# A Winograd FFN with dynamic mixing: the bias is put into PSUM by ScalarE, experts and mixing one product later

## The chip, the cores and the metric

One core of one Trainium2 chip runs the whole kernel. The metric is the device time of one launch in microseconds. The same program was run three times before the change: 948.63 us median, 948.12 to 948.87.

## The reference, cut to what matters

```python
# conditional mixing: x is (128, 64, 1024); att is (128, 8), from a small MLP on cond_128
agg_w = einsum('bk,koi->boi', att, weight)         # one 64x64 mixing matrix for each of 128 batch rows
agg_b = att @ bias_k                               # one bias for each batch row and channel
c     = einsum('boi,bih->boh', agg_w, x) + agg_b[:, :, None]
# FFN on the 8192 rows of c, 1024 columns each
logits = c @ W_router.T                            # 8 experts, top 2
h      = einsum('nd,erd->ner', c, A)               # LoRA, 8 experts of rank 16
out    = c @ W_base.T + b_base + 2 * einsum('ner,eor->no', h * combine, B)
result = x + out
```

The kernel multiplies first and mixes afterwards: `z = x @ [A | W_router | W_base].T` is 1160 columns wide, and the mixing matrix is applied to z. The bias then enters as `agg_b * col_sum`, where `col_sum` holds the sum of each of the 1160 weight columns. That product, of one value for each row and one for each column, has to be added to every mixed tile.

## The kernel before, in words

All matmuls work on fp32 split in two parts (`_hi` and `_lo`), three matmuls for one product. x is held as 64 tiles of 128 rows (two batch rows each), and two tiles make a unit: 32 units, 0 to 31. For a unit the two tiles and the two halves of the contraction make a 2x2 block matrix, and so do the weights: seven block products by Winograd's scheme (`A11`, `A12`, `S2`, `S1`, `S3`, `S4`, `A22`), each of 24 matmuls of 290 columns, in two parts. `S1` to `S4` are sums of blocks of x that VectorE makes.

The work of one unit is spread over two turns of the loop. `mix_upper(u)` at the end of turn u mixes the upper tile (side 0) of unit u into PSUM banks 4 to 6 (`O_BANK`), nine matmuls. Turn u+1 then routes it (`route`, top 2 of 8, `gate` on ScalarE for the exponential), transposes the weighted LoRA vector `hw` (`transpose_hw` on TensorE for side 0; for side 1 on TensorE in turns 1 to 4 and 31, called early, otherwise 16 block transposes on VectorE, `transpose_lower`), splits it (`hwT_high` on ScalarE, `hwT_low` on VectorE), and adds the experts (`experts`, nine matmuls into the same banks). VectorE then adds the banks to the tile's rows of `x_sb` (`result`), which frees the banks for the lower tile (`mix_lower`, side 1), and SP stores the tile.

The order on each engine is written out by hand: TensorE, ScalarE (act), VectorE (dve), GpSimd (pool) and SP each have a function `unit(u)` that lists the steps of a turn, with semaphores between the engines. Each engine takes its instructions in that order. Turn 1 is a case of its own (`first`, and `unit_1` on VectorE): there the last weight blocks `T3` and `T4` are still split, ScalarE and VectorE each with one long instruction (`split_weight`), beside the unit's other work.

The steps that the change and the prediction touch:

- `mixed` (L462 to L469) starts each bank with `start=True`; `mix_upper` and `mix_lower` (L472 to L486) wait for `out_done`, the end of `result`.
- `put_biases` (L1047 to L1051) on VectorE fills a tile's rows of `x_sb` with `col_sum * agg_b + bias_out`, when the store of the tile before has landed (`stored`); GpSimd then starts a DMA that adds x to it (`add_x`, L924 to L928).
- `route` (L992 to L1020) adds the bias to the 136 columns of logits and LoRA itself, with two `scalar_tensor_tensor`.
- The sums of products: `save` (ScalarE, PSUM to SBUF) and `add_acc` (VectorE) make `sum1`, `sum2`, `sum3`; they are split into `z_hi` (ScalarE) and `z_lo` (VectorE) by `z11_*`, `z12_*`, `z22_*`, `z21_*`. `mixed(0, 1)` in `mix_upper` needs `z12_low`.

Of the kernel before, what the change touches and what calls it, by code (L numbers as in the profile page):

```python
# [14 lines left out]
P = 128  # L15
# [87 lines left out]
def build(nc, x, xT, small, keep, mix_w, wide, b_base, bT, out):  # L103
# [8 lines left out]
    with ExitStack() as ctx:  # L112
# [10 lines left out]
        agg_b = sb("agg_b", [P, TILES])  # L123
        ones_r = sb("ones_r", [P, P], F32R)
# [54 lines left out]
        lower_hwT = sb("lower_hwT", [P, P])  # L179
# [47 lines left out]
        biased = sem("biased")  # L227
        mix_hi_done = sem("mix_hi_done")
# [22 lines left out]
        lower_hwT_made = sem("lower_hwT_made")  # L251
# [171 lines left out]
        def _(pe):  # L423
# [48 lines left out]
            def mix_upper(u):  # L472
                pe.wait_ge(mix_lo_done, tile_no(u, 0) + 1)
                pe.wait_ge(z11_lo_done, u + 1)
                mixed(0, 0).then_inc(ar_mm, 1)
                pe.wait_ge(z12_lo_done, u + 1)
                mixed(0, 1)
                mixed(0, 2).then_inc(mixed_mm, 1)

            def mix_lower(u):  # L480
                pe.wait_ge(mix_lo_done, tile_no(u, 1) + 1)
                pe.wait_ge(z22_lo_done, u + 1)
                pe.wait_ge(out_done, tile_no(u, 0) + 1)
                mixed(1, 0).then_inc(ar_mm, 1)
                mixed(1, 1)
                mixed(1, 2).then_inc(mixed_mm, 1)  # L486
# [114 lines left out]
            def unit(u, par, first=False, early=False):  # L601
# [9 lines left out]
                if first:  # L611
                    pe.wait_ge(b_lo_done, 1)
                experts(u - 1, 0)
# [5 lines left out]
                mix_lower(u - 1)  # L619
                pe.wait_ge(z11_summed, u + 1)  # L620
                pe.wait_ge(x_lo_done, splits(u, "S1"))
                product(b, "S1", True)
                pe.wait_ge(u2_saved, u)
# [7 lines left out]
                experts(u - 1, 1)  # L631
                pe.wait_ge(p5_saved, u)
                pe.wait_ge(x_lo_done, splits(u, "S4"))
                product(b, "S4", False)
                pe.wait_ge(z22_summed, u + 1)
# [4 lines left out]
                pe.wait_ge(out_done, tile_no(u - 1, 1) + 1)  # L640
# [57 lines left out]
        def _(act):  # L698
# [16 lines left out]
            def lower_hwT_high(u):  # L715

                act.wait_ge(lower_hwT_made, u * (BLOCKS * BLOCKS) - (BLOCKS_FROM - 2) * (BLOCKS * BLOCKS))
                act.wait_ge(out_mm, tile_no(u, 1))
                nc.scalar.copy(hwT_hi[:], lower_hwT[:]).then_inc(hwT_hi_done, 1)
# [107 lines left out]
            def unit(u, par, first=False, early=False):  # L827
# [8 lines left out]
                mix_high(u, 0)  # L836
                act.wait_ge(product_mm, products(u, "A11"))
                save(sum1, a, p1_saved)
                x_high("S3")
                hwT_high(2 * u - 1 if early else u + (BLOCKS_FROM - 1))  # L840
# [3 lines left out]
                act.wait_ge(s_made, sums(u, "S4"))  # L844
                act.wait_ge(product_mm, products(u, "A12"))
                x_high("S4")
                act.wait_ge(product_mm, products(u, "S2"))
                save(sum2, a, u2_saved)
                x_high("A22")
                act.wait_ge(mixed_mm, tile_no(u - 1, 1) + 1)  # L850
                mix_high(u, 1)
                if first:
                    split_weight(T4, t4_stage)
                gate(u - 1, 1)
                act.wait_ge(product_mm, products(u, "S1"))
                save(sum3, b, p5_saved)
                if early:
                    hwT_high(2 * u)
                else:
                    lower_hwT_high(u - 1)  # L860
                z11_high(u)
# [5 lines left out]
                x_high("A12")  # L867

# [12 lines left out]
            x_high("S3")  # L881
            hwT_high(LAST + (BLOCKS_FROM - 1))
            act.wait_ge(s_made, sums(u, "S4"))
# [25 lines left out]
        def _(pool):  # L909
# [34 lines left out]
            for side in range(2):  # L944
                add_x(LAST, side)

        @block.vector
        def _(dve):
# [43 lines left out]
            def route(u, side, bank=O_BANK):  # L992
# [44 lines left out]
            def result(u, side):  # L1037
# [4 lines left out]
                nc.vector.tensor_tensor(x_sb[:, side, res], ps[:, O_BANK, at], x_sb[:, side, res], ALU.add)  # L1042
# [77 lines left out]
            def unit_1():  # L1120
# [3 lines left out]
                route(0, 0)  # L1124
# [23 lines left out]
                result(0, 1)  # L1148
# [176 lines left out]
```

## Time and profile before

| what | value |
|---|---|
| median of 3 runs | 948.63 us |
| profiled execution | 948.32 us, its span 946.6 us |
| TensorE matmul busy | 939.5 us, 99% |
| VectorE busy | 777.5 us, 82% |
| ScalarE busy | 331.5 us, 35% |
| GpSimd busy | 92.8 us, 10% |
| granted TensorE clock, mean | 0.998 |

The span runs from the first to the last instruction of the profiled execution; the 1.7 us between it and the execution's time lie around it. Matmul busy times overlap (a matmul starts while the one before still drains), so the distance from one start to the next is what a matmul costs. A busy share near 100% means that there are no gaps to close.

### The profile page before, as it was taken

What the parts mean: (1) busy time and instruction counts of PE and PEld (TensorE: products, weight loads), DVE (VectorE), ACT (ScalarE), POOL (GpSimd) and SP (SyncE); (2) the same over time, 40 slices, a digit from 0 to 9 for tenths busy, and PEclk for the clock granted to TensorE, in tenths of its full rate; (3) what the DMA queues carried; (4) which work ended last, traced back from release to release, by engine and by line L of the source; (5) the groups of instructions that cost most, each with busy time, mean ns of one, the idle gap of its engine ahead of it and who ended that gap; (6) DMA issues with size and microseconds to landing.
All of it is one profiled execution on the core that took longest, in us unless ns stands there. A gap on an engine that the chain in (4) does not pass through costs nothing.

```text
span 946.6 us, 19080 instructions
## 1 busy us (share of the span) xinstructions
PE 939.5 (99%) x6713; PEld 935.7 (99%) x6713; DVE 777.5 (82%) x1970; ACT 331.5 (35%) x675; POOL 92.8 (10%) x139
## 2 busy tenths in 40 slices
PE   9999999999999999999999999999999999999997
PEld 8999999999999999999999999999999999999997
DVE  5987876888888888888888888888888888888885
ACT  6653333233332233342333332333332333332331
POOL 1111001101001101001101001100011010011010
PEclk9999999999999999999999999999999999999999
DMA  8444335444345343345344354343344343454434
GB/s 306 141 114 115 94 111 136 111 118 97 97 123 136 100 126 91 92 134 136 92 134 91 90 136 135 91 119 92 106 136 117 109 98 99 120 136 105 121 91 111
DMA packets 36053, 111.39 MB, mean 118 GB/s; under 512 B 13200, under 2 KB 13456, under 8 KB 31936
## 3 DMA queue, kind: packets, MB, share of 16 engines
q1 hardware_dynamic: 26656, 77.32, 22.3%
q0 software_dynamic: 9376, 33.78, 21.5%
q8 instruction: 14, 0.23, 0.1%
q14 instruction: 7, 0.06, 0.0%
HBM read 75.37 MB, written 35.65 MB: 117 GB/s over the span
## 4 chain that ended last, share of the span: by engine, by line
PE 98%; DMA 1%; SPq 0%; DVE 0%; ACT 0%; issue 0%; DVEq 0%
PE ps L431 25%; PE ps L435 25%; PE ps L433 25%; PE ps L491 9%; PE ps L467 4%; PE ps L465 4%; PE ps L469 4%; DMA w_stage<-in_wide 1%; PE ps L458 0%; PE ps L457 0%; PE ps L514 0%; PE ps L517 0%; SPq L371 0%; SPq L365 0%; DVE w_lo L1056 0%; DVE x_sb L1268 0%
## 5 line engine op out<-in xcount | busy, mean ns | idle before, releaser
L431 PE MATMUL ps<-w_hi,x_hi 128*128 128x290 f32 x1544 | 460.2, 298 | 0.7 <-DVE w_lo L1056 0.3
L433 PE MATMUL ps<-w_lo,x_hi 128*128 128x290 f32 x1544 | 457.8, 297 | 0.0
L435 PE MATMUL ps<-w_hi,x_lo 128*128 128x290 f32 x1544 | 456.9, 296 | 0.0
L431 PEld LDWEIGHTS ps<-w_hi,x_hi 128*128 128x128 f32 x1544 | 291.4, 189 | 2.9 <-DVE w_lo L1056 1.9
L435 PEld LDWEIGHTS ps<-w_hi,x_lo 128*128 128x128 f32 x1544 | 291.3, 189 | 0.0
L433 PEld LDWEIGHTS ps<-w_lo,x_hi 128*128 128x128 f32 x1544 | 291.2, 189 | 0.0
L700 ACT CAST x_hi<-xT_sb 128x512 fp32r<-128x512 f32 x186 | 115.5, 621 | 187.8 <-DVE xT_sb L967 167.3
L951 DVE TENSOR_TENSOR x_lo<-xT_sb,x_hi 128x512 fp32r<-128x512 f32 x186 | 129.0, 694 | 22.5 <-ACT x_hi L700 22.5
L928 POOL DMA_DIRECT2D x_sb<-in_x x64 | 55.5, 867 | 691.9 <-DVE x_sb L1049 691.9
L722 ACT COPY sum<-ps 128x580 f32<-128x580 f32 x96 | 61.6, 642 | 100.2 <-PE ps L435 100.2
L1031 DVE STREAM_TRANSPOSE lower_hwT<-hw 32x32 f32<-32x32 f32 x416 | 84.2, 202 | 12.2
L1049 DVE SCALAR_TENSOR_TENSOR x_sb<-col_sum,agg_b,bias_out 128x1024 f32<-128x1024 f32 x64 | 81.8, 1279 | 1.3 <-ACT col_sum L757 1.3
L431 PE MATMUL ps<-t_hi,x_hi 128*128 128x290 f32 x248 | 74.2, 299 | 0.0
L435 PE MATMUL ps<-t_hi,x_lo 128*128 128x290 f32 x248 | 73.9, 298 | 0.0
L433 PE MATMUL ps<-t_lo,x_hi 128*128 128x290 f32 x248 | 73.3, 296 | 0.0
L970 DVE TENSOR_TENSOR sum<-ps,sum 128x580 f32<-128x580 f32 x92 | 69.5, 755 | 1.4 <-PE ps L435 1.3
L730 ACT CAST z_hi<-sum 128x580 fp32r<-128x580 f32 x31 | 21.0, 678 | 139.0 <-DVE sum L970 139.0
L467 PE MATMUL ps<-z_hi,mix_lo 128*128 128x384 f32 x189 | 64.2, 340 | 0.0
L465 PE MATMUL ps<-z_hi,mix_hi 128*128 128x384 f32 x189 | 64.1, 339 | 0.0
L984 DVE TENSOR_TENSOR z_lo<-ps,z_hi 128x580 fp32r<-128x580 f32 x31 | 23.6, 761 | 48.8 <-ACT z_hi L735 48.8
L469 PE MATMUL ps<-z_lo,mix_hi 128*128 128x384 f32 x189 | 63.5, 336 | 0.0
L1044 DVE TENSOR_TENSOR x_sb<-ps,x_sb 128x776 f32<-128x776 f32 x62 | 59.2, 955 | 0.0
(128 smaller groups left out, 1156.4 us busy)
## 6 DMA issues: line engine op xcount, KB each, us to landing
x_sb<-in_x POOLq DMA_DIRECT2D x64, 512.0 KB, 5.4
result<-x_sb SPq DMA_DIRECT2D x63, 512.0 KB, 5.2
xT_sb<-in_xT SPq DMA_DIRECT2D x31, 1024.0 KB, 4.8
b_sb<-in_wide SPq DMA_DIRECT2D x4, 580.0 KB, 13.0
agg_w_rows<-agg_w SPq DMA_DIRECT2D x1, 2048.0 KB, 7.5
mix<-agg_w_rows SPq DMA_DIRECT2D x124, 16.0 KB, 4.4
w_stage<-in_wide SPq DMA_DIRECT2D x4, 290.0 KB, 5.4
w_stage<-in_wide SPq DMA_DIRECT2D x2, 580.0 KB, 8.0
```

Of the source, the lines that this page charges most:

```text
L431: nc.tensor.matmul(dst, x_hi[:, s, rows], high[:, c, cols], start=first, stop=False, skip_group_check=True)
L433: nc.tensor.matmul(dst, x_hi[:, s, rows], low[:, c, cols], start=False, stop=False, skip_group_check=True)
L435: mm = nc.tensor.matmul(dst, x_lo[:, s, rows], high[:, c, cols], start=False, stop=last, skip_group_check=True)
L465: nc.tensor.matmul(dst, mix_hi[:, side, :], high[:, columns(k)], start=start, stop=False, skip_group_check=True)
L467: nc.tensor.matmul(dst, mix_lo[:, side, :], high[:, columns(k)], start=False, stop=False, skip_group_check=True)
L469: return nc.tensor.matmul(dst, mix_hi[:, side, :], low[:, columns(k)], start=False, stop=True, skip_group_check=True)
L491: mm = nc.tensor.matmul(ps[:, banks[k], at], stat[:], mov[:, res], start=False, stop=True, skip_group_check=True)
L700: nc.scalar.copy(x_hi[:, SLOT[name], :], raw(name)).then_inc(x_hi_done, 1)
L951: nc.vector.tensor_tensor(x_lo[:, SLOT[name], :], raw(name), x_hi[:, SLOT[name], :].bitcast(F32), ALU.subtract).then_inc(x_lo_done, 1)
L970: nc.vector.tensor_tensor(dst[:], acc(first), dst[:], ALU.add).then_inc(done, 1)
L1031: nc.vector.transpose(lower_hwT[there, here], hw[here, there]).then_inc(lower_hwT_made, 1)
L1049: nc.vector.scalar_tensor_tensor(x_sb[:, side, :], col_sum[:, AR:WIDE], agg_b[:, bass.ds(tile_no(u, side), 1)], bias_out[:], ALU.mult, ALU.add
```

## The change

ScalarE takes over what `put_biases` did in turns 1 to 30, and in two places. It fills a tile's rows of `x_sb` with a plain copy of the output bias (`put_out_bias`), and it writes `col_sum * tile bias` into PSUM banks 4 to 6 ahead of the mixing (`seed`, in two instructions, 384 and 776 columns), so that the mixing's matmuls start with `start=False` and add to it. `take_bias` copies the tile's column of `agg_b` for it. `route` then reads logits and LoRA with plain copies. VectorE's first half of `result` signals `head_out`, so that the seed of bank 4 can go ahead of the second half. TensorE's turn has `experts(u - 1, 0)` behind `S2` instead of ahead of it, `mix_lower` behind `S1`, and `experts(u - 1, 1)` behind `S4`. The steps of ScalarE, VectorE and GpSimd are moved to fit. The unit that the prologue mixes (unit 0) and the last one keep the old way of adding the bias (`route(..., False)`, `put_biases`). The diff, without declarations and renames:

```diff
@@ -472,18 +478,25 @@
         pe.wait_ge(z11_lo_done, u + 1)
-        mixed(0, 0).then_inc(ar_mm, 1)
+        pe.wait_ge(head_put, tile_no(u, 0) - 1)
+        mixed(0, 0, start=False).then_inc(ar_mm, 1)
         pe.wait_ge(z12_lo_done, u + 1)
-        mixed(0, 1)
-        mixed(0, 2).then_inc(mixed_mm, 1)
...
-    def mix_lower(u):
+        pe.wait_ge(rest_put, tile_no(u, 0) - 1)
+        mixed(0, 1, start=False)
+        mixed(0, 2, start=False).then_inc(mixed_mm, 1)
...
+    def mix_lower(u, seeded=True):
         pe.wait_ge(mix_lo_done, tile_no(u, 1) + 1)
         pe.wait_ge(z22_lo_done, u + 1)
-        pe.wait_ge(out_done, tile_no(u, 0) + 1)
-        mixed(1, 0).then_inc(ar_mm, 1)
-        mixed(1, 1)
-        mixed(1, 2).then_inc(mixed_mm, 1)
+        if seeded:
+            pe.wait_ge(head_put, tile_no(u, 1) - 1)
+        else:
+            pe.wait_ge(out_done, tile_no(u, 0) + 1)
+        mixed(1, 0, start=not seeded).then_inc(ar_mm, 1)
+        if seeded:
+            pe.wait_ge(rest_put, tile_no(u, 1) - 1)
+        mixed(1, 1, start=not seeded)
+        mixed(1, 2, start=not seeded).then_inc(mixed_mm, 1)
@@ -608,18 +621,18 @@
         product_part(b, "A12", 1, True).then_inc(product_mm, 1)
-        if first:
-            pe.wait_ge(b_lo_done, 1)
-        experts(u - 1, 0)
         pe.wait_ge(p1_saved, u)
...
         product(a, "S2", False)
-        mix_lower(u - 1)
+        if first:
+            pe.wait_ge(b_lo_done, 1)
+        experts(u - 1, 0)
         pe.wait_ge(z11_summed, u + 1)
...
         product(b, "S1", True)
+        mix_lower(u - 1, not first)
         pe.wait_ge(u2_saved, u)
@@ -628,16 +641,15 @@
         product_part(a, "S3", 1, False).then_inc(product_mm, 1)
-        experts(u - 1, 1)
         pe.wait_ge(p5_saved, u)
...
         product(b, "S4", False)
+        experts(u - 1, 1)
         pe.wait_ge(z22_summed, u + 1)
...
         product(a, "A22", False)
-        pe.wait_ge(out_done, tile_no(u - 1, 1) + 1)
         mix_upper(u)
@@ -712,11 +724,32 @@
-    def lower_hwT_high(u):
...
-        act.wait_ge(lower_hwT_made, u * (BLOCKS * BLOCKS) - (BLOCKS_FROM - 2) * (BLOCKS * BLOCKS))
-        act.wait_ge(out_mm, tile_no(u, 1))
-        nc.scalar.copy(hwT_hi[:], lower_hwT[:]).then_inc(hwT_hi_done, 1)
+    def blocks_hwT_high(u, side, blocks):
...
+        act.wait_ge(blocks_made, blocks)
+        act.wait_ge(out_mm, tile_no(u, side))
+        nc.scalar.copy(hwT_hi[:], blocks_hwT[:]).then_inc(hwT_hi_done, 1)
...
+    def put_out_bias(u, side):
...
+        act.wait_ge(stored[side], u * 16)
+        nc.scalar.copy(x_sb[:, side, :], bias_out[:]).then_inc(out_bias_put, 1)
...
+    def take_bias(u, side):
+        nc.scalar.copy(tile_bias[:, side:side + 1], agg_b[:, bass.ds(tile_no(u, side), 1)]
+                       ).then_inc(tile_bias_done, 1)
...
+    def seed(u, side):
...
+        t = tile_no(u, side)
+        act.wait_ge(tile_bias_done, t - 1)
+        act.wait_ge(head_out, t)
+        nc.scalar.activation(ps[:, O_BANK, 0:width(0)], col_sum[:, columns(0)], ACT.Copy,
+                             scale=tile_bias[:, side:side + 1]).then_inc(head_put, 1)
+        act.wait_ge(out_done, t)
+        nc.scalar.activation(ps[:, O_BANK + 1:O_BANK + 3, 0:width(1)],
+                             col_sum[:, CUTS[1]:WIDE].rearrange("p (k n) -> p k n", k=2), ACT.Copy,
+                             scale=tile_bias[:, side:side + 1]).then_inc(rest_put, 1)
@@ -833,38 +866,49 @@
             x_high("S1")
         z22_high(u - 1)
         gate(u - 1, 0)
-        mix_high(u, 0)
         act.wait_ge(product_mm, products(u, "A11"))
         save(sum1, a, p1_saved)
+        if not first:
+            take_bias(u - 1, 1)
+        mix_high(u, 0)
         x_high("S3")
-        hwT_high(2 * u - 1 if early else u + (BLOCKS_FROM - 1))
         if first:
             act.wait_ge(t_made, T_AT["T3"])
             split_weight(T3, t_stage)
-        act.wait_ge(s_made, sums(u, "S4"))
-        act.wait_ge(product_mm, products(u, "A12"))
-        x_high("S4")
+            act.wait_ge(bias_out_in, 16)
+            act.wait_ge(agg_b_done, 2)
+            act.wait_ge(col_sum_done, 2)
+        else:
+            put_out_bias(u - 1, 1)
+        hwT_high(2 * u - 1 if early else u + (BLOCKS_FROM - 1))
         act.wait_ge(product_mm, products(u, "S2"))
         save(sum2, a, u2_saved)
+        act.wait_ge(s_made, sums(u, "S4"))
+        x_high("S4")
         x_high("A22")
-        act.wait_ge(mixed_mm, tile_no(u - 1, 1) + 1)
-        mix_high(u, 1)
         if first:
             split_weight(T4, t4_stage)
-        gate(u - 1, 1)
+        else:
+            seed(u - 1, 1)
         act.wait_ge(product_mm, products(u, "S1"))
         save(sum3, b, p5_saved)
+        gate(u - 1, 1)
+        act.wait_ge(mixed_mm, tile_no(u - 1, 1) + 1)
+        z11_high(u)
+        mix_high(u, 1)
         if early:
             hwT_high(2 * u)
         else:
-            lower_hwT_high(u - 1)
-        z11_high(u)
+            blocks_hwT_high(u - 1, 1, u * (BLOCKS * BLOCKS) - (BLOCKS_FROM - 1) * (BLOCKS * BLOCKS))
+        put_out_bias(u, 0)
+        take_bias(u, 0)
         act.wait_ge(xT_in, u * 16 + 16)
         act.wait_ge(product_mm, products(u, "S3"))
         x_high("A11")
         z12_high(u)
         act.wait_ge(product_mm, products(u, "S4"))
         x_high("A12")
+        seed(u, 0)
     units(act, unit)
     u = LAST
@@ -879,7 +923,10 @@
     x_high("S3")
+    put_out_bias(u - 1, 1)
+    take_bias(u - 1, 1)
     hwT_high(LAST + (BLOCKS_FROM - 1))
+    seed(u - 1, 1)
     act.wait_ge(s_made, sums(u, "S4"))
@@ -923,26 +970,30 @@
-        t = tile_no(u, side)
-        pool.wait_ge(biased, t + 1)
-        pool.dma_start(x_sb[:, side, :], x_tiles[t], accum_op=ALU.add).then_inc(x_in[side], 16)
+        pool.dma_start(x_sb[:, side, :], x_tiles[tile_no(u, side)], accum_op=ALU.add).then_inc(x_in[side], 16)
...
         mix_low(0, side)
+    pool.wait_ge(biased, 1)
     add_x(0, 0)
+    pool.wait_ge(biased, 2)
     add_x(0, 1)
...
         mix_low(u, 1)
+        pool.wait_ge(out_bias_put, tile_no(u, 0) - 1)
         add_x(u, 0)
+        pool.wait_ge(out_bias_put, tile_no(u, 1) - 1)
         add_x(u, 1)
...
         mix_low(LAST, side)
-    for side in range(2):
-        add_x(LAST, side)
+    pool.wait_ge(biased, 3)
+    add_x(LAST, 0)
+    pool.wait_ge(biased, 4)
+    add_x(LAST, 1)
@@ -989,16 +1040,21 @@
-    def route(u, side, bank=O_BANK):
+    def route(u, side, seeded=True, bank=O_BANK):
         t = tile_no(u, side)
...
         logits, lora = slice(ER, AR), slice(0, ER)
-        nc.vector.scalar_tensor_tensor(ar[:, logits], col_sum[:, logits], agg_b[:, bass.ds(t, 1)],
-                                       ps[:, bank, logits], ALU.mult, ALU.add).then_inc(routed, 1)
-        dve.wait_ge(routed, step + 1)
-        nc.vector.scalar_tensor_tensor(ar[:, lora], col_sum[:, lora], agg_b[:, bass.ds(t, 1)],
-                                       ps[:, bank, lora], ALU.mult, ALU.add).then_inc(routed, 1)
+        if seeded:
+            nc.vector.tensor_copy(ar[:, logits], ps[:, bank, logits]).then_inc(routed, 1)
+            dve.wait_ge(routed, step + 1)
+            nc.vector.tensor_copy(ar[:, lora], ps[:, bank, lora]).then_inc(routed, 1)
+        else:
+            nc.vector.scalar_tensor_tensor(ar[:, logits], col_sum[:, logits], agg_b[:, bass.ds(t, 1)],
+                                           ps[:, bank, logits], ALU.mult, ALU.add).then_inc(routed, 1)
+            dve.wait_ge(routed, step + 1)
+            nc.vector.scalar_tensor_tensor(ar[:, lora], col_sum[:, lora], agg_b[:, bass.ds(t, 1)],
+                                           ps[:, bank, lora], ALU.mult, ALU.add).then_inc(routed, 1)
         nc.vector.max(top_val[:], ar[:, logits]).then_inc(routed, 1)
@@ -1039,7 +1095,8 @@
         res, at = out_columns(0)
-        nc.vector.tensor_tensor(x_sb[:, side, res], ps[:, O_BANK, at], x_sb[:, side, res], ALU.add)
+        nc.vector.tensor_tensor(x_sb[:, side, res], ps[:, O_BANK, at], x_sb[:, side, res], ALU.add
+                                ).then_inc(head_out, 1)
         rest = x_sb[:, side, res.stop:D].rearrange("p (k n) -> p k n", k=2)
@@ -1131,73 +1188,68 @@
         dve.wait_ge(p1_saved, 1)
         dve.wait_ge(product_mm, products(1, "A12"))
         add_acc(sum1, b, z11_summed)
+        split_weight(T3, SPLIT_AT["T3"], t_stage)
+        x_low(1, "S3")
         result(0, 0)
-        x_low(1, "S3")
         dve.wait_ge(x_lo_done, splits(1, "A12"))
         make_s4(1)
-        split_weight(T3, SPLIT_AT["T3"], t_stage)
-        route(0, 1)
         x_low(1, "S4")
         x_low(1, "A22")
+        route(0, 1, False)
         hwT_low(0, 1)
         z11_low(1)
         dve.wait_ge(p5_saved, 1)
         dve.wait_ge(product_mm, products(1, "S3"))
         add_acc(sum3, a, z22_summed)
         split_weight(T4, SPLIT_AT["T4"], t4_stage)
-        result(0, 1)
+        dve.wait_ge(xT_in, 32)
+        make_s1(2)
         dve.wait_ge(u2_saved, 1)
         dve.wait_ge(product_mm, products(1, "S4"))
         add_acc(sum2, b, z12_summed)
-        dve.wait_ge(xT_in, 32)
-        make_s1(2)
+        result(0, 1)
         make_s3(2)
+        x_low(2, "A11")
         z12_low(1)
-        x_low(2, "A11")
         x_low(2, "A12")
         dve.wait_ge(x_lo_done, splits(2, "A11"))
-        dve.wait_ge(stored[0], 16)
         make_s2(2)
-        put_biases(1, 0)
     def unit(u, par, first=False, early=False):
         a, b = accumulators(par)
         z21_low(u - 1, b)
         route(u - 1, 0)
         x_low(u, "S2")
+        x_low(u, "S1")
+        hwT_low(u - 1, 0)
         z22_low(u - 1)
-        hwT_low(u - 1, 0)
-        x_low(u, "S1")
-        dve.wait_ge(stored[1], u * 16 - 16)
-        put_biases(u - 1, 1)
         dve.wait_ge(p1_saved, u)
         dve.wait_ge(product_mm, products(u, "A12"))
         add_acc(sum1, b, z11_summed)
-        result(u - 1, 0)
         x_low(u, "S3")
         dve.wait_ge(x_lo_done, splits(u, "A12"))
         make_s4(u)
+        result(u - 1, 0)
         x_low(u, "S4")
+        x_low(u, "A22")
         route(u - 1, 1)
-        x_low(u, "A22")
         if early:
+            z11_low(u)
             hwT_low(u - 1, 1)
         else:
-            transpose_lower(u - 1)
-            hwT_low(u - 1, 1, lower_hwT[:])
-        dve.wait_ge(stored[0], u * 16)
-        z11_low(u)
-        put_biases(u, 0)
+            transpose_blocks(u - 1, 1)
+            z11_low(u)
+            hwT_low(u - 1, 1, blocks_hwT[:])
         dve.wait_ge(p5_saved, u)
         dve.wait_ge(product_mm, products(u, "S3"))
         add_acc(sum3, a, z22_summed)
-        result(u - 1, 1)
         dve.wait_ge(xT_in, u * 16 + 16)
         make_s1(u + 1)
-        make_s3(u + 1)
         dve.wait_ge(u2_saved, u)
         dve.wait_ge(product_mm, products(u, "S4"))
         add_acc(sum2, b, z12_summed)
+        result(u - 1, 1)
+        make_s3(u + 1)
         x_low(u + 1, "A11")
         z12_low(u)
         x_low(u + 1, "A12")
@@ -1213,8 +1265,6 @@
     x_low(u, "S1")
-    dve.wait_ge(stored[1], u * 16 - 16)
-    put_biases(u - 1, 1)
     dve.wait_ge(p1_saved, u)
```

## Rows read from the trace of the kernel before

**Rows 1.** The page: busy time of the engines.
```profile
PE 939.5 (99%) x6713; PEld 935.7 (99%) x6713; DVE 777.5 (82%) x1970; ACT 331.5 (35%) x675; POOL 92.8 (10%) x139
```

**Rows 2.** All waits: waiter, whom for, us in total, times, longest.
```profile
PEld ps L514 <- DVE hw L1020: 0.2, 1, 0.2
```

**Rows 3.** Windows: turn 1, and one steady turn; stretch, busy us by engine, clock.
```profile
48.01:76.72 28.71, 28.71 (x207) 28.71 (x207) 25.02 (x50) 12.79 (x21) 2.73 (x4) 1.00 0.43 114
...
504.68:533.29 28.61, 28.61 (x207) 28.61 (x206) 24.03 (x65) 9.51 (x20) 2.69 (x4) 1.00 0.44 113
```

**Rows 4.** Timeline of ScalarE in turn 1: start us, us long, what.
```profile
51.98 0.62 ACT L700 CAST x_hi<-xT_sb 128x512 fp32r<-128x512 f32 x1
53.15 0.27 ACT L713 CAST hwT_hi<-ps 128x128 fp32r<-128x128 f32 x1 [0.55 <-PE ps L514]
53.31 2.14 ACT L746 CAST t_hi<-w_stage 128x2320 fp32r<-128x2320 f32 x1
...
61.17 2.14 ACT L746 CAST w_hi<-w_stage 128x2320 fp32r<-128x2320 f32 x1
63.20 0.20 ACT L708 ACTIVATE ratio<-top_gap 128x1 f32<-128x1 f32 x1
```

**Rows 5.** Timeline of VectorE in turn 1.
```profile
53.45 0.29 DVE L1035 TENSOR_TENSOR hwT_lo<-ps,hwT_hi 128x128 fp32r<-128x128 f32 x1 [0.80 <-ACT hwT_hi L713]
53.66 0.75 DVE L989 TENSOR_TENSOR z_lo<-sum,z_hi 128x580 fp32r<-128x580 f32 x1
54.32 1.28 DVE L1049 SCALAR_TENSOR_TENSOR x_sb<-col_sum,agg_b,bias_out 128x1024 f32<-128x1024 f32 x1
55.52 0.76 DVE L970 TENSOR_TENSOR sum<-ps,sum 128x580 f32<-128x580 f32 x1
56.26 0.42 DVE L1042 TENSOR_TENSOR x_sb<-ps,x_sb 128x248 f32<-128x248 f32 x1
56.59 0.96 DVE L1044 TENSOR_TENSOR x_sb<-ps,x_sb 128x776 f32<-128x776 f32 x1
57.46 0.68 DVE L951 TENSOR_TENSOR x_lo<-xT_sb,x_hi 128x512 fp32r<-128x512 f32 x1
58.06 0.68 DVE L967 TENSOR_TENSOR xT_sb<-xT_sb 128x512 f32<-128x512 f32 x1
58.66 2.57 DVE L1056 TENSOR_TENSOR t_lo<-w_stage,t_hi 128x2320 fp32r<-128x2320 f32 x1
61.15 0.21 DVE L997 SCALAR_TENSOR_TENSOR ar<-col_sum,agg_b,ps 128x8 f32<-128x8 f32 x1
...
63.44 0.15 DVE L1012 TENSOR_SCALAR scaled_sum<-ratio 128x1 f32<-128x1 f32 x1 [1.06 <-ACT ratio L708]
...
63.84 0.35 DVE L1020 SCALAR_TENSOR_TENSOR hw<-ar,first_w,expert_w 128x128 f32<-128x128 f32 x1
```

**Rows 6.** Timeline of TensorE in turn 1: the transposition of side 1.
```profile
65.58 0.28 PE L514 MATMUL ps<-keep_sb,hw 128*128 128x128 f32 x1
```

**Rows 7.** Timeline of ScalarE: a copy of 1024 columns.
```profile
47.16 1.05 ACT L825 CAST b_hi<-x_sb 128x1024 fp32r<-128x1024 f32 x1
```

**Rows 8.** Timelines of TensorE and its weight loads, steady turn: after the experts; `mixed(0, 1)`.
```profile
526.87 0.29 PE L431 MATMUL ps<-w_hi,x_hi 128*128 128x290 f32 x1
...
533.83 0.34 PE L465 MATMUL ps<-z_hi,mix_hi 128*128 128x388 f32 x1
...
533.65 0.19 PEld L465 LDWEIGHTS ps<-z_hi,mix_hi 128*128 128x128 f32 x1
```

**Rows 9.** Timelines of TensorE and VectorE, last turn: the last experts, and the `result` that waits.
```profile
923.92 0.64 PE L491 MATMUL ps<-b_hi,hwT_lo 128*128 128x248 f32 x3
...
924.66 0.42 DVE L1042 TENSOR_TENSOR x_sb<-ps,x_sb 128x248 f32<-128x248 f32 x1 [0.66 <-PE ps L491]
```

**Rows 10.** Timeline of VectorE, steady turn: the 16 block transposes.
```profile
521.06 3.71 DVE L1031 STREAM_TRANSPOSE lower_hwT<-hw 32x32 f32<-32x32 f32 x16
```

**Rows 11.** Groups by line: the second of ScalarE's two table loads, xcount, busy us, ns.
```profile
L780 ACT ACT_TABLE_LOAD x1 | 1.3, 1283 | 0.0
```

More of the change, by code:

```diff
@@ L123, in build @@
         agg_b = sb("agg_b", [P, TILES])
+        tile_bias = sb("tile_bias", [P, 2])
         ones_r = sb("ones_r", [P, P], F32R)
@@ L178, in build @@
         hw = sb("hw", [P, ER])
-        lower_hwT = sb("lower_hwT", [P, P])
+        blocks_hwT = sb("blocks_hwT", [P, P])
         hwT_hi = sb("hwT_hi", [P, P], F32R)
@@ L227, in build @@
         biased = sem("biased")
+        out_bias_put = sem("out_bias_put")
+        tile_bias_done = sem("tile_bias_done")
+        head_put = sem("head_put")
+        rest_put = sem("rest_put")
+        head_out = sem("head_out")
         mix_hi_done = sem("mix_hi_done")
@@ L250, in build @@
         hwT_mm = sem("hwT_mm")
-        lower_hwT_made = sem("lower_hwT_made")
+        blocks_made = sem("blocks_made")
         hwT_hi_done = sem("hwT_hi_done")
@@ L1023, in route, with transpose_blocks @@
                     expert_w[:].unsqueeze(2).to_broadcast([P, EXPERTS, RANK]), ALU.mult, ALU.mult).then_inc(hw_done, 1)
-            def transpose_lower(u):
-                dve.wait_ge(hw_done, tile_no(u, 1) + 1)
+            def transpose_blocks(u, side):
+                dve.wait_ge(hw_done, tile_no(u, side) + 1)
                 for i in range(BLOCKS):
@@ L1030, in transpose_lower @@
                         there, here = slice(j * BLOCK, (j + 1) * BLOCK), slice(i * BLOCK, (i + 1) * BLOCK)
-                        nc.vector.transpose(lower_hwT[there, here], hw[here, there]).then_inc(lower_hwT_made, 1)
+                        nc.vector.transpose(blocks_hwT[there, here], hw[here, there]).then_inc(blocks_made, 1)
             def hwT_low(u, side, whole=hwT):
@@ L1123, in unit_1 @@
                 z21_low(0, b)
-                route(0, 0)
+                route(0, 0, False)
                 dve.wait_ge(b_hi_done, 1)
@@ L1235, in _ @@
                                     ).then_inc(z21_lo_done, 1)
-            route(u, 0)
+            route(u, 0, False)
             dve.wait_ge(p5_saved, u)
@@ L1262, in _ @@
             low_half(1)
-            route(u, 1, LAST_BANKS[0])
+            route(u, 1, False, LAST_BANKS[0])
             def add_piece(side, k, bank):
```

## The prediction

> **What bounds the kernel.** I read the page first: TensorE is busy for 939.5 of 946.6 us [rows 1], VectorE for 82% and ScalarE for 35%. A busy share can hide small gaps, since matmuls overlap, so next came the windows of single turns: turn 1 takes 28.71 us and a steady turn 28.61, TensorE busy in all of it at a granted clock of 1.00 [rows 3]. A turn issues 168 matmuls of 290 columns, 18 of the mixing and 18 of the experts. From the start of S4 to `mixed(0, 1)` there are 48 of the first kind and 3 of the mixing in 6.96 us [rows 8]; 0.134 us for one of 290 columns and 0.178 for one of the mixing fit it (48 x 0.134 + 3 x 0.178 = 6.97). So a product is 3.21 us, a mixing 1.60, and the experts, which take the rest of the turn, 1.41 each. These are starts back to back. What TensorE idles in the whole span, 7.1 us [rows 1], lies in the prologue and the epilogue, which the change leaves alone. TensorE's own stream sets the time, and the change takes not one matmul out of it: the same products, the same mixing (with or without `start`), the same 38 transpositions. The 1.28 us that each `put_biases` costs VectorE [rows 5] lie beside TensorE throughout. So there is nothing to win, and the question is only whether the new order makes TensorE wait. I give places as time after the start of a turn: 48.01 for turn 1, 504.68 + 1.60 for the steady one.
>
> **Parts at nothing: TensorE's order in a steady turn.** New order: A11 0, A12 3.21, S2 6.54, experts(0) 9.75, S1 11.16, `mix_lower` 14.37, S3 15.97, S4 19.19, experts(1) 22.40, A22 23.81, `mix_upper` 27.02. For each wait I followed the other queues with the durations of before [rows 4, 5, 7] (an instruction's successor starts some 0.1 us ahead of its end: 53.66 to 54.32 for one of 0.75 us).
> ScalarE gains per turn two copies of 1024 columns (1.05 us each [rows 7]), two seeds and two `take_bias` (0.2 each, like the one-column exponential [rows 4]). The trace has no ScalarE write to PSUM. The seeds are bounded by 0.27 (128 columns) and 0.62 (512) for the 384 columns and by 0.62 and 1.05 for the 776 [rows 4, 7]; I take 0.5 and 0.85, straight between the rows. With 5.2 us more ScalarE is busy 14.7 of 28.6 us.
> Seed of the lower tile: the experts' end lets `result` start at 11.16 + 0.27 = 11.43 (the last three experts end at 924.56, VectorE starts 0.10 later [rows 9]; the next product has by then been going for 0.17). Its first half is read by 11.88, its second by 12.75 (0.42 and 0.96 long [rows 5]). Seeds end at 12.4 and 13.6; the weight loads that need them are due at 14.2 and 14.7. Margin 1.8 and 1.1 us. With the upper bounds of the seeds it is 1.7 and 0.9.
> Seed of the upper tile: behind `z12_high` and one x split, 25.05 to 26.5, due at 26.9 and 27.4. Margin about 1.
> `hw` of side 1: routing can start at 15.2 and takes 1.98 (from 61.15 to 64.19 without the 1.06 of its wait [rows 5]), so ends at 17.2; 3.7 us of block transposes [rows 10] to 20.9, `hwT_high` 21.2, due at 22.25: margin 1. `hwT_high` of side 0 is now behind `put_out_bias` and ends at 6.2, due at 9.6. In turns 2 to 4 the transposition on TensorE needs `hw` at 17.44 (17.57 less 0.13 for its weight load): margin 0.2.
> SP and GpSimd: store(0) leaves with `result` at 12.9 instead of 9.7, so the two mix loads behind it (2.2 us) push load_xT to 15.8 (before: 15.1); it lands near 21, its first users are at 22.4. The add of x for side 0 leaves at 22.2 and is wanted a turn later at 11.4; that of side 1 at 6 and is wanted at 24. GpSimd's `mix_low` is queued behind it, and is due at 27. All hidden.
> **The tightest place** is new: `result` of side 1 now stands between the last `add_acc` and `z12_low`. From A22's start: 0.27 to `result`, 0.33 + 0.87 for its halves, 0.60 `make_s3`, 0.60 `x_low`, 0.75 `z12_low` (all from starts [rows 5]), 0.04 to the next engine: 3.46. The weight load of `mixed(0, 1)` is due 3.57 after it (3.21 + 0.54 - 0.18 [rows 8]). Margin 0.1 us. I take no wait. If the chain is 0.1 longer than I think there is none yet; each 0.1 beyond costs 30 x 0.1 = 3 us. A wait that is just missed is paid at its length and no more: in the last turn the weight load of the transposition stood 0.2 us for `hw` [rows 2], and the products behind it kept their pace.
> Last turn: TensorE's order is unchanged. The lower seed ends at 10.4, due at 11.5. Nothing.
>
> **The part that costs: turn 1.** There the moves meet the two weight splits. I follow the chain from 51.98, where ScalarE's queue changes.
> ScalarE: `mix_high` (0.2), x split (0.52), then T3's split from 52.70, now ahead of `hwT_high`. A split holds the queue 2.03 us (61.17 to 63.20 [rows 4]). `hwT_high` starts at 54.73, before 53.15, and ends at 55.00.
> VectorE: `hwT_low` at 55.03 (before 53.45 [rows 5]), then by the starts of before: + 0.21 = 55.24 `z22_low`, + 0.66 = 55.90 `put_biases`, + 1.20 = 57.10 `add_acc`, + 0.68 = 57.78 T3's low half, now ahead of everything, + 2.49 = 60.27 x_low S3, + 0.60 = 60.87 `result`, + 1.20 = 62.07 `make_s4`, ready at 62.75. (The experts of side 0, done at 59.4, and `mix_lower`, which needs `result` done by 62.2, just pass.)
> ScalarE: x split S4 at 62.79 (before 58.78), x split A22 63.31, T4's split 63.83 to 65.86, the save of `sum3` 0.54, and only then `gate` of side 1: 66.40 to 66.60. Before, the gate ran at 63.20 [rows 4].
> VectorE: has routed up to the gate by 65.9, takes `scaled_sum` at 66.64, `hw` 0.40 later, done at 67.39 (0.40 and 0.35 [rows 5]).
> TensorE: the transposition of side 1 stands at the same place as before, since the steps in front are the same: 65.58 [rows 6]. It can start at 67.39 + 0.13 = 67.52 at the latest, about 1.9 us late. Behind it everything has room again (`experts(1)` needs `hwT` 5 us later, and `p5` is saved at 66.5, before S4). Next late is T4's low half, done at 72.8, wanted at 73.8. The 1.9 us stay.
>
> **Sum.** 948.32 (own time of the profiled execution: span 946.6 and 1.7 around it) + 1.9 + 0 = 950.2. The median of the runs lies 0.3 above the profiled execution, so 950.6 in the measure of the runs.
>
> **Rivals.**
> A, turn 1 absorbs the wait: if `gate` or `make_s4` comes 1.9 us earlier than my chain (it has twelve links and two are waits I inferred), the transposition is on time, and the time is 948.6, unchanged: TensorE's stream is the same. For it: margins in all other places. Against it: no link in the chain is short of its wait [rows 4, 5].
> B, `z12_low` misses in every turn: the margin is 0.1 us out of 3.57. From 0.1 us more on it decides. Port or memory contention of `put_out_bias`, the seeds and GpSimd's DMA issue beside VectorE would do it: 0.2 us more is 0.1 of wait in 30 turns, 3 us, beside turn 1: 953.6. Against it: VectorE's durations are steady (0.75 to 0.76 [rows 5] whatever runs beside).
> C, the seeds' function makes ScalarE reload its table between the exponential and the copy. One load is 1.28 us [rows 11], four a turn. The upper seed's second half would then end at 27.8 for 27.4, the routing of side 1 comes later by a load: about 0.35 us a turn, 30 turns: 950.6 + 10.5 = 961. Only two loads stand in the trace, with copies and exponentials mixed throughout; but the copies there are not activations with a scale.
> The Trainium skill (ScalarE: Activation LUTs, "Table sets: the hidden batching unit") says that cheap functions, copy among them, are in every set. By that rule there is no reload, and the trace agrees as far as it goes.
> D, faster: matmuls that run denser beside less VectorE traffic. For it: 0.134 us for 290 columns leaves room in principle. One ns on each of 6400 would give 948.6 + 1.9 - 6.4 = 944. Against it: turns with 25.0 and 24.0 us of VectorE work differ by no more than the 0.1 us of one transposition [rows 3].
>
> **Numbers.** Forecast (turn 1 alone pays) 0.60, A 0.18, B 0.15, C 0.03, D 0.04. 0.2% (1.9 us) is about what a measurement of this kernel can tell from no change, and the forecast of + 1.9 stands on that line: of its 0.60 I give 0.34 to slower, for a longer chain, and 0.26 to within. Slower 0.34 + 0.15 + 0.03 = 0.52, within 0.26 + 0.18 = 0.44, faster 0.04. The range leaves out D and C and takes in A and most of B: 948.2 to 953.8.
>
> **What would show it.** In turn 1 one wait of TensorE of 1.9 us at the transposition of side 1, released by VectorE's `hw`, the gate on ScalarE near 66.4, the turn at 30.6 us. Steady turns at 28.61 with no wait. VectorE's busy time some 60 x 1.28 = 77 us less, ScalarE's up by 150. Wrong would be: waits at `mixed(0, 1)` on `z12_low` (B), table loads in the turns (C), a wait on a seed at the mixing, or turns shorter than 28.6.

## The result

The changed kernel takes 950.77 us (median of 12 runs, 950.27 to 951.27), the kernel before, run beside it, 948.72 (948.12 to 949.42): 2.05 us more, a ratio of 1.002 with an interval of 1.0012 to 1.0028. Forecast were 950.6 us. The kernel is slower, by 0.1 to 0.3%.

The page of the changed kernel: span, and busy time of the engines.

```profile
span 949.3 us, 19345 instructions
...
PE 940.7 (99%) x6713; PEld 936.5 (99%) x6713; DVE 696.2 (73%) x1910; ACT 474.4 (50%) x915; POOL 100.1 (11%) x139
```

Against [rows 1] VectorE has 81 us less work and ScalarE 143 us more, and TensorE has as many instructions as before and waits longer. The page can't say where, the waits can. All waits of TensorE's matmuls and the first of its weight loads, columns as in [rows 2]:

```profile
PE ps L527 <- DVE hw L1076: 1.7, 1, 1.7
PE ps L549 <- POOL ones L957: 1.1, 1, 1.1
PE ps L520 <- ACT hwT_hi L725: 0.4, 1, 0.4
PE ps L437 <- DVE x_lo L1118: 0.3, 1, 0.3
PE ps L437 <- DVE sum L1021: 0.3, 1, 0.3
...
PEld ps L527 <- DVE hw L1076: 2.1, 2, 1.9
```

Behind the prologue one wait is new, the 1.7 us on `hw` (1.9 in the weight loads, whose second wait on `hw`, 0.2 us near the end, stood in the kernel before too [rows 2]). The wait on `x_lo` stands in the prologue, at 11.8 us. The windows of turn 1 and of a steady turn, which answer to [rows 3]:

```profile
48.70:79.67 30.97, 29.13 (x207) 28.69 (x207) 25.32 (x49) 14.83 (x25) 5.57 (x5) 1.00 0.51 122
507.76:536.38 28.62, 28.62 (x207) 28.62 (x206) 21.29 (x63) 14.29 (x28) 2.67 (x4) 1.00 0.43 113
```

Turn 1 takes 31.03 us from start to start of TensorE's first matmuls (48.72 to 79.75), before 28.74 (48.01 to 76.75): 2.29 us more. The steady turn is as long as before, 28.62 to 28.61, with 2.7 us less of VectorE and 4.8 us more of ScalarE in it. The two places in turn 1, from the timeline of the weight loads (the bracket is the idle time before):

```profile
63.34 0.19 PEld L471 LDWEIGHTS ps<-z_hi,mix_hi 128*128 128x128 f32 x1 [0.34 <-issue]
68.50 0.14 PEld L527 LDWEIGHTS ps<-keep_sb,hw 128*128 128x128 f32 x1 [1.94 <-DVE hw L1076]
```

The first is `mix_lower` (the profile names no releaser; VectorE's second half of `result`, which it needs, ends at 63.22), the second the transposition of side 1. ScalarE's timeline of turn 1, for [rows 4]:

```profile
52.86 0.62 ACT L712 CAST x_hi<-xT_sb 128x512 fp32r<-128x512 f32 x1
53.38 2.13 ACT L779 CAST t_hi<-w_stage 128x2320 fp32r<-128x2320 f32 x1
55.41 0.26 ACT L725 CAST hwT_hi<-ps 128x128 fp32r<-128x128 f32 x1
...
64.90 2.13 ACT L779 CAST w_hi<-w_stage 128x2320 fp32r<-128x2320 f32 x1
66.94 0.63 ACT L755 COPY sum<-ps 128x580 f32<-128x580 f32 x1
67.46 0.20 ACT L720 ACTIVATE ratio<-top_gap 128x1 f32<-128x1 f32 x1
```

And VectorE's, for [rows 5]:

```profile
55.70 0.29 DVE L1091 TENSOR_TENSOR hwT_lo<-ps,hwT_hi 128x128 fp32r<-128x128 f32 x1 [2.35 <-ACT hwT_hi L725]
...
58.45 2.70 DVE L1113 TENSOR_TENSOR t_lo<-w_stage,t_hi 128x2320 fp32r<-128x2320 f32 x1
61.08 0.94 DVE L1002 TENSOR_TENSOR x_lo<-xT_sb,x_hi 128x512 fp32r<-128x512 f32 x1
61.95 0.40 DVE L1098 TENSOR_TENSOR x_sb<-ps,x_sb 128x248 f32<-128x248 f32 x1
62.27 0.95 DVE L1101 TENSOR_TENSOR x_sb<-ps,x_sb 128x776 f32<-128x776 f32 x1
...
67.70 0.15 DVE L1068 TENSOR_SCALAR scaled_sum<-ratio 128x1 f32<-128x1 f32 x1 [0.75 <-ACT ratio L720]
...
68.10 0.35 DVE L1076 SCALAR_TENSOR_TENSOR hw<-ar,first_w,expert_w 128x128 f32<-128x128 f32 x1
```

Read from the end: `hw` waits for the gate (67.46), which stands behind T4's split and a save; the split stands behind the split of S4, which waits for `make_s4`; that stands behind T3's low half and `result` on VectorE; and these were held for 2.35 us by `hwT_low`, because `hwT_hi` stands behind T3's split on ScalarE. The spans of the two profiles differ by 2.7 us, the medians by 2.05. The 2.7 us are 0.7 in the prologue (turn 1 starts at 48.72 and not at 48.01; in all eleven profiles it starts between 48.0 and 48.9), 2.3 in turn 1, 0.2 in turns 2 to 30 together, and 0.5 less from the start of turn 31 to the end (39.27 to 39.74). Whether the last one belongs to the change is not shown: the nine profiles in the new order have 39.15 to 39.48 there, the two in the old order 39.62 and 39.74.

### The profile page after: what moved, and what is told of

Read it like the earlier page. It is cut to its first block, busy times and chain, and to the rows that moved or that the text cites. A ratio compares the mean times of both kernels' runs of the same rounds, so it can differ in the third digit from the quotient of the medians.

```text
span 949.3 us, 19345 instructions
## 1 busy us (share of the span) xinstructions
PE 940.7 (99%) x6713; PEld 936.5 (99%) x6713; DVE 696.2 (73%) x1910; ACT 474.4 (50%) x915; POOL 100.1 (11%) x139
## 4 chain that ended last, share of the span: by engine, by line
PE 96%; DVE 1%; DMA 1%; ACT 1%; issue 0%; SPq 0%; DVEq 0%
PE ps L441 25%; PE ps L437 25%; PE ps L439 25%; PE ps L504 9%; PE ps L473 3%; PE ps L475 3%; PE ps L471 3%; DMA w_stage<-in_wide 1%; PE ps L464 0%; PE ps L463 0%; PE ps L527 0%; ACT w_hi L779 0%; PE ps L530 0%; SPq L377 0%; ACT x_hi L712 0%
## 5 line engine op out<-in xcount | busy, mean ns | idle before, releaser
L712 ACT CAST x_hi<-xT_sb 128x512 fp32r<-128x512 f32 x186 | 112.4, 621 | 6.6 <-DVE xT_sb L1018 4.8
L1087 DVE STREAM_TRANSPOSE blocks_hwT<-hw 32x32 f32<-32x32 f32 x416 | 84.4, 203 | 13.1
L1098 DVE TENSOR_TENSOR x_sb<-ps,x_sb 128x248 f32<-128x248 f32 x62 | 25.8, 416 | 85.4 <-PE ps L504 85.2
L968 POOL TENSOR_TENSOR mix_lo<-mix,mix_hi 128x128 fp32r<-128x128 f32 x64 | 50.3, 787 | 302.0 <-ACT mix_hi L716 302.0
L736 ACT COPY x_sb<-bias_out 128x1024 f32<-128x1024 f32 x60 | 62.8, 1047 | 0.0
L750 ACT ACTIVATE ps<-col_sum,tile_bias 128x776 f32<-128x776 f32 x60 | 54.8, 913 | 9.3 <-DVE x_sb L1101 7.5
```

The source lines that it names most:

```text
L712: nc.scalar.copy(x_hi[:, SLOT[name], :], raw(name)).then_inc(x_hi_done, 1)
L736: nc.scalar.copy(x_sb[:, side, :], bias_out[:]).then_inc(out_bias_put, 1)
L1087: nc.vector.transpose(blocks_hwT[there, here], hw[here, there]).then_inc(blocks_made, 1)
```

## The experiments

Unless told otherwise an experiment starts from the changed kernel. Each ratio is to runs of the kernel before taken beside the experiment, with medians between 948.66 and 948.92; differences to the changed kernel are between medians taken apart, and the traces' turns, given below, are the finer measure. "Back" means as in the kernel before.

**t1_transpose_first**, ScalarE's turn 1, one step back:

```diff
+                    hwT_high(2 * u - 1)
                     act.wait_ge(t_made, T_AT["T3"])
                     split_weight(T3, t_stage)
...
                 else:
                     put_out_bias(u - 1, 1)
-                hwT_high(2 * u - 1 if early else u + (BLOCKS_FROM - 1))
+                    hwT_high(2 * u - 1 if early else u + (BLOCKS_FROM - 1))
```

> The changed kernel with one step of ScalarE's turn 1 put back: the copy of the transposed LoRA vector (hwT_high of side 0) again ahead of T3's split. Theory (turn 1 alone pays, by the queue of ScalarE and VectorE): VectorE's queue runs 1.6 us earlier up to result of side 0, which then waits for the experts until 59.5 (on the clock of the old trace); gate of side 1 near 65.0, hw near 66.0, TensorE waits 0.5 us at the transposition instead of 1.7, and not at all at mix_lower: 1.5 us less than the changed kernel, about 949.3 us, ratio to the kernel before 1.0006. Rival (the wait in turn 1 is hidden elsewhere and the loss is spread over the steady turns): 950.8 us as the changed kernel, whatever turn 1 does.

949.77 us (949.17 to 949.99), ratio 1.0008 (0.9999 to 1.0017). That is 1.0 us less than the changed kernel, not 1.5. No wait at `mix_lower`, but 0.95 us at the transposition, where I had 0.5. The theory holds against its rival. A term of 0.4 us is missing in my chain: `hw` ends 18.37 us after the start of the turn, and I had 18.0 (66.0 less 48.01).

**t1_gate_only**, the other step alone:

```diff
+                if first:
+                    gate(u - 1, 1)
                 act.wait_ge(product_mm, products(u, "S1"))
                 save(sum3, b, p5_saved)
-                gate(u - 1, 1)
+                if not first:
+                    gate(u - 1, 1)
```

> The changed kernel with only the gate of side 1 put ahead of the save of sum3 in turn 1; hwT_high stays behind T3's split. Theory (one chain through ScalarE and VectorE sets hw, its terms add): the save's 0.54 us comes off the chain and nothing else, 0.5 us less than the changed kernel, 950.2 us; with the 1.0 us that putting hwT_high back gave it makes up the 1.6 of both. Rival (the save is hidden by another link, and what t1_both_back gained beyond t1_transpose_first was noise): 950.8 us.

950.16 us, ratio 1.0014 (1.0004 to 1.0023; one of its 11 runs took 2367 us, which hardly moves the median). 0.6 us less; the wait at the transposition is 1.40 instead of 1.94, 0.54 less, which is the save's step.

**t1_both_back**, both edits:

> As the one before, and in turn 1 gate of side 1 also ahead of the save of sum3 (0.54 us). Theory: hw is there within 0.1 us of its transposition, TensorE waits at most 0.1 us in turn 1, the time is that of the kernel before: 948.7 us, ratio 1.000 (0.9995 to 1.0005). Rival (spread loss): 950.8 us, ratio 1.002.

949.20 us (948.23 to 949.87), ratio 1.0003 (0.9994 to 1.0012). 1.6 us are gone with two moved steps in one of 31 turns. The weight load of the transposition still stands for a moment:

```profile
66.43 0.14 PEld L527 LDWEIGHTS ps<-keep_sb,hw 128*128 128x128 f32 x1 [0.42 <-DVE hw L1080]
```

Its waits in the four kernels go 1.94, 1.40, 0.95, 0.42: the gate's step takes 0.54 off each time, the other 1.0. The terms add, so one chain sets this wait. The step of `hwT_high` also ends the 0.34 us at `mix_lower`. Turn 1 shows both, from start to start of TensorE's first matmuls:

| kernel | turn 1, us | waits in it, us |
|---|---|---|
| before | 28.74 | none |
| changed | 31.03 | 0.34 + 1.94 |
| t1_gate_only | 30.50 | 0.34 + 1.40 |
| t1_transpose_first | 29.64 | 0.95 |
| t1_both_back | 29.14 | 0.42 |

So `hwT_high`'s place is worth 1.4 us and the gate's 0.5 us. The turns behind do not move: turns 5 to 30 take 28.62 us each in all four kernels with the new order.

**mix_low_early**, one GpSimd instruction moved:

```diff
             add_x(0, 0)
+            mix_low(1, 0)
             pool.wait_ge(biased, 2)
...
-                mix_low(u, 0)
+                if not first:
+                    mix_low(u, 0)
```

> The changed kernel, its turn 1 as it is, with one GpSimd instruction moved: mix_low of unit 1's upper tile ahead of the add of x that waits for put_biases. In the changed kernel it runs at 58.75 for 2.72 us beside VectorE's low half of T3 (2.70 us instead of 2.57) and x_low S3 (0.94 instead of 0.68). Theory (the two slow each other, and in turn 1 that lies on the chain): moved to 53 to 54, where VectorE waits for hwT_hi, it takes 0.5 to 0.8 us, T3's low half 2.57 and x_low 0.68; result comes 0.4 us earlier, TensorE no longer waits at mix_lower (0.34 us now) and waits 0.4 us less for side 1 in all: 950.4 us against 950.77. Rival (the long rows are a matter of what is read, not of GpSimd): the same durations and 950.8 us.

950.29 us (950.00 to 950.73), ratio 1.0015: 0.5 us less than the changed kernel. Turn 1 takes 30.63 us, 0.40 less. GpSimd's timeline in the changed kernel, in this one, and VectorE's in this one:

```profile
58.75 2.72 POOL L968 TENSOR_TENSOR mix_lo<-mix,mix_hi 128x128 fp32r<-128x128 f32 x1
68.51 0.46 POOL L968 TENSOR_TENSOR mix_lo<-mix,mix_hi 128x128 fp32r<-128x128 f32 x1 [7.04 <-ACT mix_hi L716]
```

```profile
52.66 0.64 POOL L968 TENSOR_TENSOR mix_lo<-mix,mix_hi 128x128 fp32r<-128x128 f32 x1 [2.41 <-ACT mix_hi L716]
```

```profile
51.75 1.22 DVE L1185 TENSOR_TENSOR b_lo<-x_sb,b_hi 128x1024 fp32r<-128x1024 f32 x1
...
58.06 2.56 DVE L1115 TENSOR_TENSOR t_lo<-w_stage,t_hi 128x2320 fp32r<-128x2320 f32 x1
60.54 0.68 DVE L1004 TENSOR_TENSOR x_lo<-xT_sb,x_hi 128x512 fp32r<-128x512 f32 x1
```

The three rows are short again (2.72 to 0.64, 2.70 to 2.56, 0.94 to 0.68), and the 0.34 us at `mix_lower` are gone. (The moved instruction does not run quite alone: `b_lo` is still on VectorE until 52.97. The second row of the changed kernel, 0.46 us, is the same instruction for the other tile, with VectorE idle beside it.) The wait at the transposition stayed (1.91): TensorE and `hw` both come 0.4 us earlier in the turn. "0.4 us less in all" held.

**pad_128** and **pad_512** start from t1_both_back and put one unused VectorE instruction in turns 2 to 30 into the chain that I had called the tightest place:

```diff
                 result(u - 1, 1)
+                nc.vector.tensor_tensor(spare[:], ar[:, 0:128], ar[:, 0:128], ALU.add)
                 make_s3(u + 1)
```

(pad_512 adds 512 columns of `bias_out` to themselves.)

> The kernel with turn 1 put back, and in turns 2 to 30 one more VectorE instruction (128 columns, 0.20 us from start to start, result unused) between result of side 1 and make_s3, in the chain to z12_low. Theory (margin of 0.13 us there, read off the changed kernel's trace as 0.11 to 0.16): each of 29 turns gets 0.07 us longer, 2 us in all: 950.7 us. Rival 1 (the margin is larger, the weight load can come later than I read it): 948.7. Rival 2 (the chain is already late in each turn): 0.20 x 29 = 5.8 us, 954.5.

> The same with 512 columns (0.60 us from start to start). Theory: 0.60 - 0.13 = 0.47 us in each of 29 turns, 13.6 us: 962.3 us; TensorE's wait stands at mixed(0, 1), released by z12_low. Rival 1 (margin twice as large, 0.3): 8.7 us, 957.4. Rival 2 (none): 17.4 us, 966.1. The difference to pad_128 is 0.4 us a turn, 11.6 us, by theory and rival 2, less by rival 1.

950.10 us (949.41 to 950.76) and 962.05 us (961.56 to 962.22). Against t1_both_back that is 0.9 us, 0.03 a turn for a step of 0.20, and 12.85 us, 0.44 a turn for a step of 0.60. The traces agree: turns 5 to 30 take 28.653 and 29.067 us, 0.033 and 0.447 more than the 28.620 of t1_both_back. The margin, step less loss, is 0.15 to 0.17 us; I had 0.13 from the trace. Rivals 1 and 2 fall. The waits of pad_512:

```profile
PE ps L472 <- DVE z_lo L1035: 4.8, 29, 0.2
...
PEld ps L472 <- DVE z_lo L1035: 14.0, 29, 0.5
```

29 waits, in 29 turns. The matmuls' rows show only 4.8 of the 13 us, the weight loads' 14.0: matmuls are still draining while the next weight load already waits.

**blocks_both_sides** starts from t1_both_back and uses what the change freed on VectorE. From turn 5 on side 0 is transposed in blocks too:

```diff
-                transpose_hw(u - 1, 0)
+                if early:
+                    transpose_hw(u - 1, 0)
...
                 x_low(u, "S1")
-                hwT_low(u - 1, 0)
-                z22_low(u - 1)
+                if early:
+                    hwT_low(u - 1, 0)
+                    z22_low(u - 1)
+                else:
+                    transpose_blocks(u - 1, 0)
                 dve.wait_ge(p1_saved, u)
                 dve.wait_ge(product_mm, products(u, "A12"))
                 add_acc(sum1, b, z11_summed)
+                if not early:
+                    hwT_low(u - 1, 0, blocks_hwT[:])
+                    z22_low(u - 1)
```

> Turn 1 put back as in t1_both_back, and from turn 5 on VectorE transposes side 0 in 16 blocks too, with the time that the change freed on it: between x_low S1 and add_acc, with hwT_low and z22_low behind add_acc; TensorE's transposition of side 0 goes. Theory (TensorE's stream alone sets the time, VectorE's 3.7 us more fit): each of 26 turns loses one transposition of 0.11 us, 2.9 us: 946.3 us, turns of 28.51. Rival (VectorE has no room at that place: z11_summed or hwT late for S1 or the experts): no gain or a loss, 949 us or above, waits of TensorE in each turn.

945.75 us (945.46 to 945.91), ratio 0.9968 (0.9956 to 0.998): 2.9 us less than the kernel before and 3.45 less than t1_both_back, where 2.9 were expected. A turn of it:

```profile
504.10:532.60 28.50, 28.50 (x206) 28.50 (x205) 24.29 (x79) 14.35 (x28) 2.68 (x4) 1.00 0.43 112
```

One matmul fewer and still no gap. Over turns 5 to 30 the mean turn is 28.507 us against 28.620, 0.113 less, and 26 turns give the 2.9 us expected. The other 0.5 us between the medians lie within the spread of the runs (0.3 of them if each is taken against its own runs of the kernel before).

**blocks_from_3**, the same with `BLOCKS_FROM = 3`:

> The same with the block transposes from turn 3 on instead of turn 5 (the written-out turns 3 and 4 go into the loop). Theory: two more turns without two transpositions on TensorE, 4 x 0.11 = 0.4 us less than blocks_both_sides: 945.9 us. Rival (the first turn of the loop pays for its jump or its code, which turns 3 and 4 as straight code did not): no gain against blocks_both_sides, 946.3 or more.

945.89 us (945.56 to 946.35), ratio 0.9971 (0.996 to 0.9982). The medians show no gain where 0.4 was expected. The trace shows the gain and what hides it: turns 2 to 4 take 85.73 us together instead of 86.17, which is the 0.44, and turn 1 starts at 48.91 instead of 48.34. The prologue has one wait more than its sister's, 0.5 us on `agg_w`, in a part that the edit doesn't touch. The rival (a price at the entry of the loop) is not seen in the turns. Why the prologue is later, and whether it is so in every run, stays open.

**old_order_blocks** makes the same attempt on the kernel before: blocks for side 0, `put_biases` still on VectorE and the experts behind A12.

```diff
                 route(u - 1, 0)
+                if not early:
+                    transpose_lower(u - 1, 0)
                 x_low(u, "S2")
...
+                    hwT_low(u - 1, 0, lower_hwT[:])
+                    z22_low(u - 1)
```

> The kernel before with the same block transposes of side 0 from turn 5 on, right behind route of side 0, and everything else in the old order (put_biases on VectorE, experts behind A12). It shows what the change is good for. Theory (in the old order the experts of side 0 stand 6.5 us into the turn, hw is there at 3.5, 3.7 us of block transposes make hwT 1.2 us late; result then ends 0.2 us late for mix_lower, and side 1's hwT comes 1.0 us late for its experts): 2.4 - 0.1 us a turn, 26 turns: about 1009 us. Rival (VectorE, with 27.7 us of work in 28.6, has its idle time at the right places and absorbs it): 946 to 950 us.

1027.4 us, ratio 1.0829 (1.0812 to 1.0845): 3.0 us a turn, where I had 2.3. The weight loads of a turn:

```profile
519.14 0.41 PEld L491 LDWEIGHTS ps<-b_hi,hwT_hi 128*128 128x128 f32 x3 [1.35 <-ACT hwT_hi L720]
524.14 0.19 PEld L465 LDWEIGHTS ps<-z_hi,mix_hi 128*128 128x128 f32 x1 [0.35 <-issue]
533.46 0.42 PEld L491 LDWEIGHTS ps<-b_hi,hwT_hi 128*128 128x128 f32 x3 [1.26 <-ACT hwT_hi L720]
```

The three places are the three expected ones (1.2, 0.2 and 1.0); each is 0.15 to 0.26 us longer, 0.6 together; another 0.1 to 0.2 us of the turn is in none of the three rows. So the change pays for itself only with the next step, the 3.7 us of transposes. Two things in it make room for them: it moves the experts 3.2 us back from their routing, and it takes two 1.28 us instructions off VectorE. No run tells what each is worth, and this run has the transposes one step earlier in VectorE's queue than blocks_both_sides has.

## Why the prediction was right

- *TensorE's stream sets the time, nothing to win in steady turns.* Right. 28.62 to 28.61 us a turn, no wait. Rival D (denser matmuls beside less VectorE traffic) has nothing in it: VectorE went from 24.0 to 21.3 us a turn, and the turn did not get shorter (28.613 to 28.620 us over turns 5 to 30).
- *Turn 1 pays.* Right in place and chain, and shown by putting the two steps back. Counted from the turn's start, the gate stands at 18.74 (forecast 18.39) and `hw` ends at 19.73 (19.38). The chain was 0.35 us short, and this is the one term of the sum that was mis-sized. I had taken T3's low half at 2.49 and x_low at 0.60, from rows where GpSimd was idle; it was late itself, behind an add of x that waits for `put_biases`, and ran beside them: from start to start they took 2.63 and 0.87. The same 0.35 us is also the first wait: I wrote that `result` "just passes" `mix_lower`, and it missed by 0.34. TensorE was then itself 0.34 late at the transposition, so the wait there is 1.94 as in my sum, and the whole is 1.94 + 0.34 = 2.28 us in the trace instead of 1.9.
- *The measured total.* 2.05 us between the medians, 0.15 more than the 1.9 of the forecast, where turn 1 alone is 2.29 longer. In the traces something gives back part of it: 0.5 us behind the start of turn 31. That 950.6 came so near to 950.77 is thus in part luck, since the chain was short by more than the total shows.
- *Seeds at nothing.* Right, with the price a little low: 0.585 us for 384 columns and 0.912 for 776, where I had 0.5 and 0.85, inside the bounds.

Columns: start, duration, of the upper tile's seeds in a steady turn.

```profile
505.47 0.58 ACT L747 ACTIVATE ps<-col_sum,tile_bias 128x384 f32<-128x384 f32 x1
506.12 0.92 ACT L750 ACTIVATE ps<-col_sum,tile_bias 128x776 f32<-128x776 f32 x1
```

The second ends at 507.04, and the weight load that needs it comes at 508.11: 1.07 us of margin (forecast: about 1). Rival C (table loads) did not come: there are two table loads in the whole trace, as before.
- *The tightest place.* The trace of the changed kernel, VectorE and the weight load of `mixed(0, 1)`:

```profile
504.79 0.42 DVE L1098 TENSOR_TENSOR x_sb<-ps,x_sb 128x248 f32<-128x248 f32 x1 [0.46 <-PE ps L504]
...
507.20 0.76 DVE L1030 TENSOR_TENSOR z_lo<-sum,z_hi 128x580 fp32r<-128x580 f32 x1
```

```profile
508.11 0.19 PEld L471 LDWEIGHTS ps<-z_hi,mix_hi 128*128 128x128 f32 x1
```

`z12_low` ends at 507.96, 0.15 us ahead. The forecast of 0.1 was near, no turn missed it, and the pads measured it as 0.15 to 0.17. With 0.20 us more in the chain (pad_128) rival B's wait comes, but at 0.03 us a turn, a third of its price. One argument against B was wrong: that VectorE's durations are steady whatever runs beside. In turn 1 one of 0.68 us took 0.94.
- *The chances.* The forecast stood on the line of 0.2%, and so did the result: it is clearly not zero (1.0012 to 1.0028), and on which side of 0.2% it lies these runs can't tell. What they rule out is B's spread loss.

## What to carry to other kernels

Where one engine runs without gaps, price a reordering by each wait's margin, and first in the turns that are not like the others: here 30 turns took the new order at almost no cost, and one turn, with two long splits in the queues, paid 2 us. A chain across two in-order engines is worth writing out link by link; a term is missing where a third engine is moved beside it. Work taken off an engine that doesn't set the time is worth only what the next edit puts there: the change cost 2 us, and with turn 1 put back and side 0's transposition on VectorE the kernel takes 945.75 us, with blocks_from_3 (945.89) the fastest seen here.

## What the runs showed of the hardware

- GpSimd and VectorE slow each other, and GpSimd suffers far more. One 128x128 subtraction on GpSimd took 2.72 us beside a long VectorE subtraction, 0.64 us where VectorE was busy with another for the first 0.31 us, and 0.46 us beside an idle VectorE; VectorE's 2320 columns took 2.70 instead of 2.56 us and its 512 columns 0.94 instead of 0.68. The Trainium skill (GPSIMD Engine Reference, "Specifications") lists GpSimd's SBUF interfaces as shared with VectorE, with contention when a VectorE instruction has two SBUF inputs, as both of these have; mix_low_early agrees.
- ScalarE writes a scaled tile of 128 rows to PSUM in 0.27 us + 0.834 ns a column (from 0.585 us at 384 and 0.912 at 776). The Trainium skill (ScalarE: Activation LUTs, "What ACT_TABLE_LOAD costs") has about 280 ns + 0.833 ns a column for an activation with one pointer operand; the trace agrees within 0.02 us.
- A late operand costs TensorE about what its weight load waits, and no more. In turn 1 waits of 0.34 and 1.94 us made the turn 2.29 us longer; in pad_512 29 waits of 0.48 us made each turn 0.45 us longer. The granted clock stayed at 1.00.
